# One product for the last gate and up columns of a shared network, and the queues around it

## The reference

```
# x: 2048 tokens x 256; sw_gate, sw_up: 256 x 704; sw_down: 704 x 256
sh = silu(x @ sw_gate) * (x @ sw_up) @ sw_down
sh = sigmoid(x @ w_shared_gate) * sh
out = experts(x) + sh
```

## Time and profile before

| what | us |
|---|---|
| median of 3 runs | 1159.09 (1157.61 to 1159.81) |
| the profiled execution, own time | 1157.37 |
| its span, first to last instruction | 1155.7 |
| TensorE busy in the span | 1042.3 (90%) |
| VectorE busy | 945.5 (82%) |
| ScalarE busy | 892.8 (77%) |

### The profile page before, as it was taken

How to read it: one execution, slowest core, us unless ns; L and a number is a source line. 1 busy time by engine, 2 the same in 40 slices (tenths; PEclk the granted TensorE clock), 3 DMA queues, 4 the chain that set the end, 5 groups by cost and what they waited for, 6 DMA issues and landing times.

```text
span 1155.7 us, 24019 instructions
## 1 busy us (share of the span) xinstructions
PE 1042.3 (90%) x8274; PEld 602.8 (52%) x8388; DVE 945.5 (82%) x1732; ACT 892.8 (77%) x1546; POOL 700.7 (61%) x625
## 2 busy tenths in 40 slices
PE   8988888888888888888888888999999999999997
PEld 4744444444444444444444446756654465557775
DVE  6999999999999999999999996963327888943335
ACT  4799999999999999999999997645533576834441
POOL 3027888888787888888788877247751000653432
PEclk9999999999999999999999999999999999999999
DMA  6799998888798788887875775847928002523336
GB/s 195 123 177 139 174 172 161 170 171 172 167 174 169 169 167 175 172 158 164 170 116 110 115 107 92 261 143 213 325 99 329 1 1 52 175 89 106 101 94 235
DMA packets 388799, 176.36 MB, mean 153 GB/s; under 512 B 330413, under 2 KB 373650, under 8 KB 388680
## 3 DMA queue, kind: packets, MB, share of 16 engines
q1 hardware_dynamic: 381976, 157.85, 63.1%
q0 software_dynamic: 6480, 16.77, 4.3%
q10 hardware_dynamic: 224, 0.20, 0.1%
HBM read 52.70 MB, written 43.59 MB: 83 GB/s over the span
## 4 chain that ended last, share of the span: by engine, by line
PE 46%; DVE 27%; ACT 15%; issue 6%; POOL 3%; DMA 2%; SPq 0%; ACTq 0%; POOLq 0%; DVEq 0%
DVE top L425 21%; ACT weight L485 11%; PE bank L234 7%; PE bank L220 7%; PE bank L1206 4%; PE bank L2641 4%; PE bank L1605 3%; PE bank L252 3%; PE bank L2657 3%; PE bank L1193 2%; PE bank L1182 2%; POOL weight L537 1%; PE bank L684 1%; PE bank L1878 1%; PE bank L1623 1%
## 5 line engine op out<-in xcount | busy, mean ns | idle before, releaser
L485 ACT ACTIVATE weight<-bank,bias,sq_all 128x1024 uint8<-128x1024 f32 x512 | 610.1, 1201 | 14.0 <-PE bank L234 8.8
L425 DVE TENSOR_REDUCE top<-bank 128x1 f32<-128x512 f32 (+1 forms) x683 | 610.2, 951 | 11.2 <-PE bank L220 0.9
L537 POOL CAST weight<-turned 128x2048 bf16<-128x2048 uint8 x256 | 479.5, 1895 | 39.0 <-DMA turned<-weight 19.3
L234 PE MATMUL bank<-kT,query 128*128 128x512 bf16 x918 | 284.2, 381 | 26.9 <-ACT weight L485 12.8
L252 PEld LDWEIGHTS bank<-v_sb,weight 128*128 128x128 bf16 x4096 | 172.1, 97 | 104.7 <-POOL weight L537 2.9
L220 PE MATMUL bank<-kT,qspace 64*128 64x512 bf16 x687 | 134.9, 386 | 55.9 <-DVE top L425 55.9
L252 PE MATMUL bank<-v_sb,weight 128*128 128x16 bf16 x4096 | 172.5, 169 | 2.2 <-POOL weight L537 1.8
L220 PE MATMUL bank<-kT,query 128*128 128x512 bf16 x329 | 124.8, 379 | 2.1 <-DVE top L425 1.4
L234 PEld LDWEIGHTS bank<-kT,query 128*128 128x128 bf16 x1024 | 59.7, 96 | 104.2 <-ACT weight L485 62.0
L1848 POOL DMA_INDIRECT dispatched_rows<-qspace,put x32 | 37.2, 1162 | 116.0 <-DVE qspace L2398 106.9
L485 ACT ACTIVATION_READ_ACCUMULATOR weight<-bank,bias,sq_all 128x1 f32 x512 | 101.3, 198 | 0.0
(11 more groups left out here) (351 smaller groups left out, 1459.2 us busy)
## 6 DMA issues: line engine op xcount, KB each, us to landing
dispatched_rows<-zeros SPq DMA_DIRECT2D x32, 524.0 KB, 3.2
answered_rows<-zeros SPq DMA_DIRECT2D x16, 512.0 KB, 3.2
late<-answered_rows SPq DMA_DIRECT2D x16, 512.0 KB, 6.7
erow<-dispatched_rows SPq DMA_DIRECT2D x39, 131.0 KB, 2.1
wgu<-in_L_ffn_w_gate SPq DMA_DIRECT2D x26, 176.0 KB, 3.7
wgu<-in_L_ffn_w_up SPq DMA_DIRECT2D x26, 176.0 KB, 3.6
query<-qspace SPq DMA_DIRECT2D x32, 128.0 KB, 3.2
turned<-weight SPq DMA_TRANSPOSE x256, 3.2
```

Of the source, the lines that this page charges most:

```text
L234: mm = pe.matmul(unit[u % 2][:, v * 512:(v + 1) * 512], query2[:, t % 2, h, :], kT[:, h // 2, first + v * 512:first + (v + 1) * 512], star ...
L425: ve.tensor_reduce(top[:, first:first + count], bank[:, first % 3:first % 3 + count, :], AX.X, ALU.max).then_inc(s_max, 1)
L485: ac.activation(weight8[:, n % BYTES, u * 1024:(u + 1) * 1024], unit[u], ACT.Exp, bias=bias[:, n:n + 1], scale=sq_all[:, n:n + 1], accum_o ...
L537: po.tensor_copy(weight[:, n % 3, :, :, :].rearrange("p c q two -> p (c q two)"), turned8[:, n % 3, :, :].rearrange("p c q -> p (c q)").bi ...
```

## The change

- The last 64 gate columns and the last 64 up columns lie side by side as 128 weight columns, `swb`. One product of full width puts the gate's 64 rows on partitions 0 to 63 and up's 64 rows on partitions 64 to 127 of the gate's bank. There is no `up` product of chunk 5 in any group.
- silu of chunk 5 reads partitions 0 to 63 and writes partitions 64 to 127 of `sil`; the product with up, `hT[:, 5]` and the last down weights lie on partitions 64 to 127.
- The weights of `sw` are loaded in six transfers in place of four.
- The gate's bank is now read by VectorE too. The next group's first gate product waits for `hidden_ready`, and so do silu of the next group's first chunk, and the first of the second network's.
- VectorE takes chunk 5 before chunk 4 in groups 1 to 3, with what stood between them now between them in the new order.
- On TensorE the gate product of chunk 1 of groups 2 and 3 moves behind the first answers or the turned keys, and in group 3 the chunk 5 product moves ahead of chunk 4's up product.

```diff
-            swg = sw[:, 0:CK * FS0].rearrange("p (c n) -> p c n", c=CK)
-            swu = sw[:, CK * FS0:2 * CK * FS0].rearrange("p (c n) -> p c n", c=CK)
+            LAST, HALF = NW0 - 1, slice(FS0 % P, 2 * (FS0 % P))
+            WHOLE = LAST * P
+            swg = sw[:, 0:CK * WHOLE].rearrange("p (c n) -> p c n", c=CK)
+            swu = sw[:, CK * WHOLE:2 * CK * WHOLE].rearrange("p (c n) -> p c n", c=CK)
+            swb = sw[:, 2 * CK * WHOLE:2 * CK * FS0].rearrange("p (c n) -> p c n", c=CK)
+            rows_of = [slice(0, w) for w in WID0[:LAST]] + [HALF]
...
# shared_gate_tensor
+                if c == 0 and i > 1:
+                    pe.wait_ge(sm_["hidden_ready"], n - 1)
                 for k in range(CK):
-                    mm = pe.matmul(bank[0:w, gate_bank(n), :], swg[:, k, c * P:c * P + w], xT[:, k, g * 512:(g + 1) * 512], start=k == 0, stop=k == CK - 1)
+                    weights = swb[:, k, :] if c == LAST else swg[:, k, c * P:c * P + w]
+                    mm = pe.matmul(bank[0:P, gate_bank(n), :], weights, xT[:, k, g * 512:(g + 1) * 512], start=k == 0, stop=k == CK - 1)
...
# shared_answers_tensor
-                        mm = pe.matmul(bank[:, 6 + k % 2, 0:C], hT[0:w, c, k * P:(k + 1) * P], swd[0:w, c, :], start=c == 0, stop=c == NW0 - 1)
+                        mm = pe.matmul(bank[:, 6 + k % 2, 0:C], hT[rows_of[c], c, k * P:(k + 1) * P], swd[rows_of[c], c, :], start=c == 0, stop=c == NW0 - 1)
...
# shared_scalar
-                        ac.wait_ge(sm_["hidden_ready"], n - 1)
-                    ac.activation(sil[0:w, n % 2, :], bank[0:w, gate_bank(n), :], ACT.Silu).then_inc(sm_["gates_passed"], 1)
+                        ac.wait_ge(sm_["hidden_ready"], n if c == 0 else n - 1)
+                    ac.activation(sil[rows_of[c], n % 2, :], bank[0:w, gate_bank(n), :], ACT.Silu).then_inc(sm_["gates_passed"], 1)
...
# shared_hidden_vector
-                    ve.wait_ge(sm_["up_products"], n + 1)
+                    if c < LAST:
+                        ve.wait_ge(sm_["up_products"], i * LAST + c + 1)
...
-                    ve.tensor_tensor(hT[0:w, c, :], sil[0:w, n % 2, :], bank[0:w, up_bank(n), :], ALU.mult).then_inc(sm_["hidden_ready"], 1)
+                    r = rows_of[c]
+                    ve.tensor_tensor(hT[r, c, :], sil[r, n % 2, :], bank[r, up_bank(n) if c < LAST else gate_bank(n), :], ALU.mult).then_inc(sm_["hidden_ready"], 1)
...
# front_sync
-                sp.dma_start(swg, a["L0_ffn_sw_gate"].rearrange("(c p) n -> p c n", p=P)).then_inc(s_wf, 16)
-                sp.dma_start(swu, a["L0_ffn_sw_up"].rearrange("(c p) n -> p c n", p=P)).then_inc(s_wf, 16)
+                for n, (columns, whole) in enumerate((("L0_ffn_sw_gate", swg), ("L0_ffn_sw_up", swu))):
+                    columns = a[columns].rearrange("(c p) n -> p c n", p=P)
+                    sp.dma_start(whole, columns[:, :, 0:WHOLE]).then_inc(s_wf, 16)
+                    sp.dma_start(swb[:, :, n * (P // 2):(n + 1) * (P // 2)], columns[:, :, WHOLE:]).then_inc(s_wf, 16)
...
# front_tensor
                 gate0(5)
                 fill_table(2)
-                up0(5)
                 fill_table(3)
...
# second_gate_tensor, the second network's first gate product
+                        if g == 0 and c == 0:
+                            pe.wait_ge(sm_["hidden_ready"], n - 1)
...
# mixing_tensor
                         shared_gate_tensor(pe, 2, 2, 0)
-                        shared_up_tensor(pe, 1, 1, 5)
-                        shared_gate_tensor(pe, 2, 2, 1)
                         pe.wait_ge(sx_["answers_weighted"], E0)
                         shared_answers_tensor(pe, 1, 1, 0, 1)
+                        shared_gate_tensor(pe, 2, 2, 1)
                         turn_keys(0)
...
                         shared_gate_tensor(pe, 3, 3, 0)
-                        shared_up_tensor(pe, 2, 2, 5)
-                        shared_gate_tensor(pe, 3, 3, 1)
                         keys_taken(0)
                         turn_keys(1)
+                        shared_gate_tensor(pe, 3, 3, 1)
                         shared_answers_tensor(pe, 2, 2, 0, 1)
...
                         turn_mixed(1)
+                        shared_gate_tensor(pe, 3, 3, 5)
                         shared_up_tensor(pe, 3, 3, 4)
-                        shared_gate_tensor(pe, 3, 3, 5)
                         logits_taken(0)
                         places(0)
-                        shared_up_tensor(pe, 3, 3, 5)
                         second_gate_tensor(pe, 0, 0)
...
# mixing_scalar, silu of the second network
-                            ac.wait_ge(sm_["hidden_ready"], n - 1)
+                            ac.wait_ge(sm_["hidden_ready"], n if g == 0 and c == 0 else n - 1)
...
# mixing_vector
                         combine(1, 4)
+                        hidden0(1, 5)
+                        first_statistics(0)
                         hidden0(1, 4)
-                        first_statistics(0)
-                        hidden0(1, 5)
...
                         offsets(1, "first")
+                        hidden0(2, 5)
+                        second_statistics(0)
                         hidden0(2, 4)
-                        second_statistics(0)
-                        hidden0(2, 5)
                         combine(3, 8)
...
                         add_mixed(1)
+                        hidden0(3, 5)
+                        sum_keys(2)
                         hidden0(3, 4)
-                        sum_keys(2)
-                        hidden0(3, 5)
                         second_statistics(1)
```

More of the change, by code:

```diff
@@ L1340, in front_tensor @@
                 turn_rows(pe, 2)
-                pe.wait_ge(s_wf, 64)
+                pe.wait_ge(s_wf, 96)
                 gate0(0)
@@ L2445, in second_hidden @@
                             ve.wait_ge(sm_["gates_passed"], n + 1)
-                            ve.wait_ge(sm_["up_products"], n + 1)
+                            ve.wait_ge(sm_["up_products"], NG * LAST + NW1 * g + c + 1)
                             if c == 0 and g > 0:
@@ L2584, in half_fetched @@
                             return s_got[i], 16 * G + 16
-                        event, loads = ((s_td, 2), (s_wf, 4), (s_wn, 1), (s_wr, 2))[i - NG]
+                        event, loads = ((s_td, 2), (s_wf, 6), (s_wn, 1), (s_wr, 2))[i - NG]
                         return event, 16 * loads + 16
```

2 lines of the change are left out of this document (1 added, 1 removed).

## The result

The changed kernel takes 1168.37 us (median of 6 executions, 1166.24 to 1169.30), the kernel before 1158.27 in the same session (6 executions). The ratio is 1.0086, with an interval of 1.0075 to 1.0096: slower by 10.1 us. The direction was forecast, the size was not: 1163.5 us with a range to 1166.5.

The account below looks back on a forecast made before the run. TensorE was busy 90% of the span, but at the changed places ScalarE or VectorE was taken to arrive last. Delays of 0 + 1.6 (containing group 1's 0.7) + 2.8 gave +4.4 us, a median of 1163.5, range 1160 to 1166.5.

Parts of the forecast that it names:

- The front, D = 0: Before group 1: without up(0,5) TensorE still waits for VectorE's marking at fill_table(3), loads arrive in time; delay 0.
- The waits: New TensorE pauses of 3.0, 3.0 and 2.4 us ahead of gate(2,0), turn_keys(1) and answers(3,0); delay +4.4 us in all.
- group 1: gate(2,0) waits for hidden(1,5) behind VectorE's second addition; TensorE idles 3.0 us, delay +0.7 us.
- group 2: turn_keys(1) waits for ScalarE's normalising behind silu(3,0); TensorE idles 3.0 us, delay +1.6 us including group 1's 0.7.
- group 3: hidden(3,5), now ahead of sum_keys(2), waits for silu(3,5); answers(3,0) wait for all of hidden, +2.8 us more.
- The price of a product: A removed up(i,5) on TensorE was worth 1.86 + (1.92 - 1.72) = 2.06 us.
- ScalarE's shifted silu: Chunk 5's silu reading partitions 0 to 63 and writing 64 to 127: taken as 0, upper end +1.8 us.
- By the row alone no fall is due: Clock held some 3.3 us after TensorE's last work, so new pauses of 3.0, 3.0 and 2.4 us bring no fall.
- rival C: The clock falls in a pause and work there takes double: 2 to 5 us more, 1165.5 to 1168.5; chance 0.12.
- Rival A: TensorE stays the bound, so groups 2, 3 and one more give 2.06 us each: faster, 1153; chance 0.07.
- B: VectorE's reordering in group 3 is hidden as silu(3,5) arrives by 955; only +1.6 remains, 1160.7; chance 0.13.
- D: As a rival: late weights or a slow shifted silu, +1 to +2.5 us, 1164.5 to 1166; chance 0.08.

Follow-up runs that it names:

- e5: The changed kernel with TensorE products of unused result filling all four pauses (front, groups 1, 2 and 3): 1163.42 us.
- e8: The changed kernel with the edits of e6 and e7, group 1's orders mended, and gate(1,0) and silu(1,0) put into the front's pause: 1153.72 us.
- e3: The changed kernel with group 3's VectorE order as before, the second network's first gate waiting for all of hidden: 1168.27 us.
- e4: The changed kernel with gate(3,1) moved back ahead of turn_keys(1) in TensorE's queue: 1164.78 us.
- e6: The changed kernel with group 2 reordered: ScalarE normalises the keys ahead of silu(3,0), VectorE makes hidden(2,4) ahead of the statistics: 1162.78 us.
- e7: The changed kernel with group 3 reordered: gate(3,5), silu(3,5) and hidden(3,5) earlier, sum_keys(2) behind hidden(3,4), two table loads fewer: 1162.04 us.
- e9: e8 without its step in the front, gate(1,0) and silu(1,0) standing in group 1 again: 1154.92 us.
- e1: The changed kernel with TensorE products of unused result filling the pauses in the front and groups 2 and 3: 1164.57 us.
- e2: The changed kernel with 2 TensorE products of unused result filling the front's pause alone: 1165.07 us.
- e10: e8 with the joint product's halves changed over, up columns on partitions 0 to 63, gate columns on 64 to 127: 1152.80 us.
- e11: The kernel before, products separate, with e8's ScalarE and VectorE reorderings in groups 1 to 3 as far as allowed, no front filling: 1163.03 us.
- e13: The kernel of e10 measured once more, unchanged, beside e12: 1154.42 us.
- e12: e10 with two TensorE products of unused result in each of the two pauses left in group 1: 1153.73 us.

## Why the prediction was wrong

- **The front, D = 0.** Right for the loads: gate(0,0) starts at 737.17, to the hundredth. Right that fill_table(3) waits for VectorE's marking (767.07 for 767.08). Wrong in what it took the pause to be worth: nothing. The removed product had kept TensorE busy; without it the pause is 2.54 us, and the half clock stood behind it for the answers (13.68 for 12.00 us), of which about 1 reached group 1. This pause is missing from the forecast's list of new ones.
- **The waits.** The three that were listed came in their place and with their releaser, and the sums held: 5.2 for 4.4, group 1 1.0 for 0.7, group 2 1.3 for 0.9, group 3 2.9 for 2.8. The working also had the second network's first gate wait for hidden(3,5), 0.5 us later than before, but did not see that with up(3,5) gone this is a pause of 2.99 us. Part of what the sums missed is the 64-row step on partitions 64 to 127, priced at nothing by the nearest form: 0.1 to 0.2 us each time on VectorE. That it accounts for the rest in after is worked out and not shown. ScalarE's shifted silu added nothing on the path: from silu(3,5) to hidden(3,5) it is 0.62 us before and after.
- **The price of a product.** The forecast took 1.92 for the full product behind a 64-wide one from the chain of waits, where the next piece starts later than on TensorE's own timeline; start to start it is 1.82 (915.85 to 917.67), so 1.96 and not 2.06. Nothing hangs on it: the sum did not use it.
- **The step that failed is the clock**: "By the row alone no fall is due." The row at the kernel's end showed a clock that held for some 3.3 us of idleness, and I read a safe bound out of one instance, with pauses of 3.0, 3.0 and 2.4 close below it. The clock fell behind 2.5, 3.3 and 3.0 with 2.3, and lay low long enough to cost 6.3 us by the rows, 5.6 by e5's trace and 4.6 by its median. That is rival C, and its mechanism; it had 0.12. The measured 1168.37 lies at the upper end of C's 1165.5 to 1168.5, in part by luck: C started from 1159.09 for the kernel before, not 1158.27, and its 2 to 5 us counted one tile of answers at the half clock where more than two of the three ran so (3.36 us), and left the front out. The rule it cites, from "TensorE: Matmul & The Clock Gate" of the Trainium skill (idle gaps between bursts bring the half clock), agrees with the trace of after at three places and not at group 1's pause of 3.22 us, behind which the clock stayed.
- **Rival A** was dismissed for the right reason: at both places another engine arrives last. e8 shows that it is true of the queues as written and not of the product: with the orders mended, the kernel is faster by 4.2 us.
- **B and D** did not happen: group 3's reordering wasn't hidden, and the weights came in time.

## What to carry to other kernels

Work taken from an engine that is then the one to wait buys a pause, and a pause costs more than its length when TensorE's clock falls behind it: price every new pause of the sizes seen here (2 us and more) at the half clock too, 1.7 or 3.4 us of TensorE's work, as a chance and not as a yes or no, or put real work into it. List the pauses that the removal itself opens, not only those that new waits bring. When a product goes away, go through the neighbouring engines' queues and mend their order in the same change; here that turned +10 us into -4. And hold a mended order against the old kernel too: an order that pays with one set of products can cost 5 us with another.

## What the runs showed of the hardware

- The clock fell behind the front's pause of 2.5 us in each of the six profiled executions that had it (after, e3, e4, e6, e7, e9), behind group 1's 3.2 in e1, e2, e3 and e6 and not in after, e4 and e7, behind group 2's 3.3 in after, e3 and e7 and not in e2, and at group 3's 3.0 or 5.0 in all five that had it (after, e2, e3, e4, e6). Behind two shorter pauses in group 1, the second of 1.96, it fell in e8, e10, e11 and e13 and not in e9. It also fell where no pause was longer than about 1.2 us: near 736 us in e5, e11, e12 and e13, and at 784 in e12.
- The granted clock between 700 and 1050 us, in steps of 1 us, shows 27 falls in 14 of the 15 traces (none in before). In 22 of them a TensorE that is busy throughout loses 1.7 us (12.00 us of work take 13.68), in five it loses 3.4 (after, e4 and e6 in group 3, e6 in group 1, e13 near 736; 8.91 take 12.27).
- Executions of one kernel differ with this. Of the kernel before, those at a mean clock of 0.998 took 1156.4 to 1156.9 us, those at 0.994 to 0.997 1157.9 to 1159.1 (13 executions beside e5 to e8).
- A 64-row step of VectorE that reads and writes partitions 64 to 127, between steps from partition 0, overlaps its neighbours less: the next one starts 0.72 us behind it in place of 0.61. ScalarE's silu of 64 rows that writes to 64 to 127 is followed by the next ACTIVATE after 0.61 in place of 0.49; reading its input from 64 to 127 cost nothing.
